# A graph layer with normalisation on one core: two of three row pairs turned by VectorE instead of every second one, block transfers issued from two queues, every sixth pair normalised by VectorE

## The chip, the core and the metric

The kernel runs on one core of one Trainium2 chip. The metric is the device time of one execution in microseconds, taken as the median of several runs. TensorE (PE in the profile), VectorE (DVE), ScalarE (ACT), GpSimd (POOL) and SyncE (SP) each follow an instruction queue of their own and meet only at semaphores. Data moves between HBM and the on-chip memory on 16 DMA engines.

## The reference, cut to what matters

There are 50,000 nodes with 512 float32 features. `src` and `dst` hold 62,500 edges sorted by `dst`: every node has a loop onto itself, and 12,500 edges join other nodes.

```
def _L0_gnn_ref(x, edge_index, W_l, W_r, b):
    src, dst = edge_index[0], edge_index[1]
    msg = x[src]
    agg = segment_sum(msg, dst, num_segments=n)
    deg = segment_sum(ones, dst, num_segments=n)
    mean = agg / maximum(deg, 1.0)[:, None]
    h = mean @ W_l + b + x @ W_r
    return h * sigmoid(h)
x = _layernorm(x + _L0_gnn_ref(x, (src, dst), W_l, W_r, b), axis=-1)   # eps 1e-5
```

A node whose only edge is its loop has mean = x, so that h = x @ (W_l + W_r) + b. For the others the kernel adds a correction row, computed from the differences x[src] - x[dst].

## The kernel before, in words

The rows are worked on in tiles of 128. The products are float32: the data and the weights are each split into a high and a low part of type float32r, and a tile of 128 rows takes 12 matmuls of 512 columns (four chunks of 128 features by three products, `three` at L529, issued at L535).

There are three stages. **Early** (to about 220 us): the products of the first 44 tiles (EARLY) are computed and kept in HBM, while VectorE sorts out which edges are not loops. **Edges** (to about 500 us): 98 tiles of correction rows (ET) are computed and written to HBM. **Node pairs** (from about 500 us): the other 347 tiles go by in 174 pairs (NP) of 256 rows, the last with 80 rows only. Between them the early tiles, called light, are finished, one for every four pairs.

All engines run a loop `node_pair(t)` (or `serve`, `move`) written out over t, with a fixed order of steps and with the steps of neighbouring pairs shifted against each other. For pair t:

- SP loads the rows into `X`, four buffers (`load_x`, L326), as soon as the residual of the pair four before has been added (`u_made`), and it stores the output (`store_out`, L344) when `normed` says so. `O` has two buffers, freed by `stored`.
- GpSimd gathers the correction rows of the pair into `cor`, four buffers (`gather_cor`, L468), over a bias that ScalarE has written there first (`reset_cor`, L747). Rows without a correction are skipped.
- The contracted feature must lie on the partitions, so x is turned. For even t TensorE does it: eight transposes of 128x128 into PSUM (`transpose_x`, L628, issued at L639), at the start of iteration t-1. For odd t VectorE does it in blocks of 32x32: SP loads the same rows a second time in another arrangement (`load_blocks`, L336: four DMAs, one for each 32 partitions, in runs of 128 elements, 512 bytes), into `x_raw`, and VectorE turns them into `x_blocks` with one instruction (`turn_blocks`, L1096). There is one buffer of each; both lie in `xs`, which the edge stage used for its gathers. The weights for these pairs have their rows in the matching order (`wb_hi`, `wb_lo`). `by_blocks` (L206) says which pair goes which way, and `turned_by_pe` (L209) counts the others.
- ScalarE rounds the turned rows to `x_hi` (`round_x`, L786: L792 from blocks, L796 from PSUM), and VectorE makes `x_lo` as the difference (`split_x`, L1083: L1088 and L1091).
- ScalarE copies the gathered corrections into PSUM (`seed`, L810), and TensorE accumulates 24 matmuls onto them.
- ScalarE applies SiLU from PSUM into `Z` (L833), VectorE adds X (`residual`, L1117) and takes mean and variance (`moments`, L1125 and L1128), GpSimd computes 1/sqrt(var + eps) (`make_rstd`, L502 and L505), VectorE makes -mean*rstd (`make_shift`, L1135), and ScalarE writes O = Z*rstd + shift in two instructions (`normalise`, L806).

The order in an iteration t on ScalarE is silu(t-1), round_x(t+1), seed(t+1), reset_cor(t+3), light steps, normalise(t-3); on VectorE moments(t-2), split_x(t+1), residual(t-1), make_shift(t-2), light steps, turn_blocks(t+2); on SP load_blocks(t+3), load_x(t+3), store_out(t-3), light transfers; on TensorE the transposes of t+1, then the 24 matmuls of t; on GpSimd a light rstd, make_rstd(t-2), gather_cor(t+3), a light gather.

## Time and profile before

| | |
|---|---|
| median of three runs | 1539.95 us (1539.58 to 1540.2) |
| the profiled execution, its own time | 1544.13 us |
| its span, first to last instruction | 1542.3 us |
| TensorE busy | 97% of the span |
| VectorE, ScalarE, GpSimd busy | 85%, 77%, 66% of the span |
| granted TensorE clock, mean | 0.993 |
| DMA | 397.68 MB, 258 GB/s over the span |

The profiled execution is one run of its own, 4.2 us longer than the median of the three others. Busy shares are means over three stages with different limits, so a change in the node stage is to be read from windows of that stage. TensorE's busy time counts matmuls from their start to a modelled end, and they overlap; the time from one to the next is shorter than the duration printed.

### The profile page before, as it was taken

How to read it: one execution, taken by the hardware profiler on the slowest of the kernel's cores; microseconds unless marked ns; L12 is line 12 of the kernel's file. 1: busy time of each engine (PE TensorE's matmuls, PEld its weight loads, DVE VectorE, ACT ScalarE, POOL GpSimd, SP SyncE). 2: the span in 40 equal slices, each digit the busy share in tenths (PEclk: the TensorE clock that was granted, in tenths of full speed). 3: DMA queues.
4: the chain of work that ended last, by engine and by line, in shares of the span. 5: the costliest groups of instructions: out<-in, count | busy, mean ns of one | idle time of the engine just before them, and what ended most of it. 6: DMA issues, size and time to landing. Idle time of an engine off the chain costs nothing.

```text
span 1542.3 us, 23969 instructions
## 1 busy us (share of the span) xinstructions
PE 1501.2 (97%) x7198; PEld 1241.7 (81%) x7198; DVE 1317.7 (85%) x2090; ACT 1180.2 (77%) x1603; POOL 1019.6 (66%) x1089
## 2 busy tenths in 40 slices
PE   7989999999999999999999999999999999999996
PEld 6868778887888778888888888888888888888885
DVE  7977999998998778888878888888888888888886
ACT  4444333433334689999999999999999999999997
POOL 6436556665662767777767767676777776777774
PEclk9999999999999999999999999999999999999998
DMA  5466588987898689999999999999999999999996
GB/s 192 149 209 196 173 248 256 272 257 241 266 266 250 182 254 292 275 285 282 272 266 275 287 289 270 282 287 273 285 276 279 276 277 282 286 268 284 279 279 199
DMA packets 299349, 397.68 MB, mean 258 GB/s; under 512 B 43036, under 2 KB 145206, under 8 KB 299221
## 3 DMA queue, kind: packets, MB, share of 16 engines
q1 hardware_dynamic: 251239, 321.43, 69.4%
q0 software_dynamic: 46944, 74.22, 17.8%
q8 instruction: 58, 0.95, 0.3%
q14 instruction: 70, 0.57, 0.1%
q10 hardware_dynamic: 1038, 0.50, 0.1%
HBM read 333.87 MB, written 139.67 MB: 307 GB/s over the span
## 4 chain that ended last, share of the span: by engine, by line
PE 68%; issue 9%; ACT 7%; DMA 6%; DVE 5%; POOL 3%; SPq 1%; POOLq 0%; ACTq 0%; DVEq 0%
PE pH L535 62%; DMA cor<-correction_rows,node_idx 3%; PE pT L639 3%; PE pT L608 2%; ACT cor L753 2%; ACT O L806 2%; POOL cor L441 1%; ACT pH L821 1%; ACT Z L833 1%; DMA xs<-in_x 1%; PE pT L546 1%; DVE stats L1125 1%; POOL var_eps L502 1%; SPq L310 1%; POOL rstd L505 1%
## 5 line engine op out<-in xcount | busy, mean ns | idle before, releaser
L441 POOL DMA_INDIRECT cor<-correction_rows,node_idx x347 | 397.5, 1146 | 242.9 <-ACT cor L753 144.3
L535 PE MATMUL pH<-ws_hi,x_hi 128*128 128x512 f32 x876 | 346.9, 396 | 5.8 <-ACT pH L821 2.0
L535 PE MATMUL pH<-ws_hi,x_lo 128*128 128x512 f32 x876 | 342.9, 391 | 0.0
L535 PE MATMUL pH<-ws_lo,x_hi 128*128 128x512 f32 x876 | 342.0, 390 | 0.0
L535 PE MATMUL pH<-wb_hi,x_hi 128*128 128x512 f32 x688 | 275.6, 401 | 1.4 <-DVE x_lo L1088 1.3
L535 PE MATMUL pH<-wb_hi,x_lo 128*128 128x512 f32 x688 | 268.2, 390 | 0.0
L535 PE MATMUL pH<-wb_lo,x_hi 128*128 128x512 f32 x688 | 267.8, 389 | 0.0
L806 ACT ACTIVATE O<-Z,shift,rstd 128x512 f32<-128x512 f32 x347 | 262.0, 804 | 2.0 <-DVE shift L1135 1.9
L1125 DVE BATCH_NORM_STATS2 stats<-Z 128x6 f32<-128x512 f32 x347 | 219.3, 673 | 0.0
L1117 DVE TENSOR_TENSOR Z<-Z,X 128x1024 f32<-128x1024 f32 x174 | 211.2, 1214 | 1.1 <-ACT Z L833 1.1
L727 ACT ACTIVATE s_hi<-sums 128x512 fp32r<-128x512 f32 x98 | 62.0, 633 | 189.9 <-issue 141.4
L535 PEld LDWEIGHTS pH<-ws_hi,x_hi 128*128 128x128 f32 x876 | 164.8, 188 | 43.0 <-issue 9.2
L535 PEld LDWEIGHTS pH<-ws_hi,x_lo 128*128 128x128 f32 x876 | 164.8, 188 | 35.2
L505 POOL TENSOR_TENSOR rstd<-var_eps,minus_half 128x2 f32<-128x2 f32 x174 | 183.3, 1054 | 14.5
L535 PEld LDWEIGHTS pH<-ws_lo,x_hi 128*128 128x128 f32 x876 | 165.1, 188 | 32.8
L833 ACT ACTIVATE Z<-pH 128x1024 f32<-128x1024 f32 x170 | 172.4, 1014 | 20.6 <-PE pH L535 18.6
L753 ACT ACTIVATE cor<-bias_rows 128x1024 f32<-128x1024 f32 x174 | 182.8, 1051 | 0.0
L821 ACT ACTIVATE pH<-cor 128x1024 f32<-128x1024 f32 x170 | 172.9, 1017 | 10.8 <-DMA cor<-correction_rows,node_idx 10.4
L1091 DVE TENSOR_TENSOR x_lo<-pT,x_hi 128x1024 fp32r<-128x1024 f32 x88 | 106.9, 1215 | 82.0 <-issue 56.7
L535 PE MATMUL pH<-wl_hi,s_hi 128*128 128x512 f32 x392 | 163.3, 417 | 2.7 <-DVE s_lo L1043 1.8
L441 POOL DMA_INDIRECT xd<-in_x,dst_idx x98 | 99.9, 1019 | 95.3 <-issue 69.6
L535 PE MATMUL pH<-wl_hi,s_lo 128*128 128x512 f32 x392 | 155.6, 397 | 0.0
(145 smaller groups left out, 2751.4 us busy)
## 6 DMA issues: line engine op xcount, KB each, us to landing
X<-in_x SPq DMA_DIRECT2D x173, 512.0 KB
out<-O SPq DMA_DIRECT2D x173, 512.0 KB
xs<-in_x SPq DMA_DIRECT2D x344, 128.0 KB
correction_rows<-c_out SPq DMA_DIRECT2D x98, 256.0 KB
light_x<-in_x SPq DMA_DIRECT2D x58, 256.0 KB, 2.8
light_h<-early_product SPq DMA_DIRECT2D x44, 256.0 KB
out<-light_o SPq DMA_DIRECT2D x44, 256.0 KB
join_row<-joined SPq DMA_DIRECT2D x98, 64.0 KB
```

The costliest lines, as they stand in the source:

```text
L441: g.indirect_dma_start(out=out_, out_offset=None, in_=table, in_offset=bass.IndirectOffsetOnAxis(ap=idx, axis=0), bounds_check=bound, oob_ ...
L505: g.tensor_tensor(rstd[0:rows, b, 0:nt], var_eps[0:rows, b, 0:nt], minus_half[0:rows, 0:nt], ALU.pow).then_inc(rstd_made, 1)
L535: last = mm(ps, a[:, k], w[:, k], start=(n == 0 and not onto), stop=(n == len(terms) - 1), skip_group_check=onto)
L639: last = nc.tensor.transpose(pT[u % 2][:, a, k * P:k * P + rows], X[0:rows, b, a, k * P:(k + 1) * P], eye[0:rows, 0:rows])
L727: a_(s_hi[b][:], sums[:, b, :, 2:], ACT.Copy).then_inc(s_hi_made, 1)
L753: a_(cor[u][:], bias_rows[:].rearrange("p (a n) -> p a n", a=1).to_broadcast([P, 2, D]), ACT.Copy).then_inc(cor_reset, 1)
L806: last = a_(O[0:rows, b, a], Z[0:rows, u % 4, a], ACT.Identity, scale=rstd[0:rows, b, a:a + 1], bias=shift[0:rows, b, a:a + 1])
L821: a_(pH[u % 2][0:rows, 0:nt], cor[b][0:rows, 0:nt], ACT.Copy).then_inc(seeded, 1)
L833: a_(Z[0:rows, b, 0:nt], h, ACT.Silu).then_inc(silu_made, 1)
L1091: v.tensor_tensor(x_lo[b][:, :, 0:nt, 0:rows].rearrange("p k a r -> p a k r"), pT[b][:, 0:nt].rearrange("p a (k r) -> p a k r", k=K)[:, :, ...
L1117: v.tensor_tensor(Z[0:rows, b, 0:nt], Z[0:rows, b, 0:nt], X[0:rows, b, 0:nt], ALU.add).then_inc(u_made, 1)
L1125: v.bn_stats(stats[0:rows, u % 2, a], Z[0:rows, u % 4, a]).then_inc(stats_made, 1)
```

## The change

1. Two of three pairs (t not a multiple of 3, and not the last) are turned by VectorE; the others and the last by TensorE.
2. `x_raw` and `x_blocks` have two buffers each, used in turn (`block_ring`); the second lies in `xd`, which becomes one tensor. `blocks_in` becomes two semaphores.
3. Of the four block DMAs of a pair, SP issues those of partitions 0 to 63, and ScalarE, between `seed` and `reset_cor`, those of partitions 64 to 127.
4. Pairs with t a multiple of 6 are normalised by VectorE, with (Z - mean) * rstd in two `tensor_scalar` instructions, ahead of `turn_blocks`; they need no shift. Some waits on `shift_made` and `rstd_made` become waits on `normed`.

```diff
@@ -91,8 +91,8 @@
         xs = sb("xs", [P, 4, D], f32)
-        x_raw, x_blocks = xs[:, 0:2], xs[:, 2:4]
-        xd = [sb(f"xd{b}", [P, D], f32) for b in range(4)]
+        xd = sb("xd", [P, 4, D], f32)
+        x_raw, x_blocks = (xs[:, 0:2], xd[:, 0:2]), (xs[:, 2:4], xd[:, 2:4])
         diff = [sb(f"diff{b}", [P, D], f32) for b in range(2)]
@@ -174,7 +174,7 @@
         cor_in = [sem(f"cor_in{b}") for b in range(4)]
-        blocks_in, blocks_turned = sem("blocks_in"), sem("blocks_turned")
+        blocks_in, blocks_turned = [sem(f"blocks_in{b}") for b in range(2)], sem("blocks_turned")
         transposed, hi_made, lo_made, product, z_made, silu_made = (sem("transposed"), sem("hi_made"), sem("lo_made"),
@@ -204,10 +204,28 @@
         def by_blocks(t):
-            return t % 2 == 1 and t < NP - 1
+            return t % 3 != 0 and t < NP - 1
         def turned_by_pe(t):
-            return t // 2 + 1 + t // (NP - 1)
+            return sum(not by_blocks(p) for p in range(t + 1))
+
+        def turned_by_dve(t):
+            return sum(by_blocks(p) for p in range(t + 1))
+
+        def block_ring(t):
+            n = turned_by_dve(t) - 1
+            return n % 2, n // 2
+
+        def normed_by_dve(t):
+            return t % 6 == 0
+
+        def shifts(t):
+            return sum(not normed_by_dve(p) for p in range(t + 1))
+
+        def block_part(t, j):
+            first = BASE + 2 * t * P
+            return (x_raw[block_ring(t)[0]][32 * j:32 * j + 32].rearrange("r a (i c) -> r (a i) c", i=4),
+                    x[first:first + 2 * P, j * P:(j + 1) * P].rearrange("(i r) c -> r i c", r=32))
@@ -334,12 +352,9 @@
             def load_blocks(t):
-                wait(sp, blocks_turned, (t + 1) // 2 - 1)
-                first = BASE + 2 * t * P
-                for j in range(4):
-                    sp.dma_start(x_raw[32 * j:32 * j + 32].rearrange("r a (i c) -> r (a i) c", i=4),
-                                 x[first:first + 2 * P, j * P:(j + 1) * P].rearrange("(i r) c -> r i c", r=32)
-                                 ).then_inc(blocks_in, 16)
+                wait(sp, blocks_turned, turned_by_dve(t) - 2)
+                for j in range(2):
+                    sp.dma_start(*block_part(t, j)).then_inc(blocks_in[block_ring(t)[0]], 16)
@@ -379,6 +394,7 @@
                     load_blocks(1)
+                    load_blocks(2)
             peeled(0, ET, edge_tile)
@@ -497,7 +513,6 @@
                 wait(pool, mv_made, 2 * t + 2)
-                wait(pool, shift_made, t - 1)
                 wait(pool, normed, t - 1)
@@ -631,8 +646,8 @@
                 pe.wait_ge(x_in[b], 16 * (used + 1))
-                if fixed(t) and t < 2:
-                    pe.wait_ge(sums_made, ET - 1 + t)
+                if fixed(t) and t < 4:
+                    pe.wait_ge(sums_made, min(ET - 1 + t, ET))
                 wait(pe, lo_made, t - 1)
@@ -788,8 +803,8 @@
                 if by_blocks(t):
-                    act.wait_ge(blocks_turned, (t + 1) // 2)
-                    a_(in_blocks(x_hi[b]), x_blocks.rearrange("p a (i k r) -> p (a i) k r", k=K, r=32), ACT.Copy
+                    act.wait_ge(blocks_turned, turned_by_dve(t))
+                    a_(in_blocks(x_hi[b]), x_blocks[block_ring(t)[0]].rearrange("p a (i k r) -> p (a i) k r", k=K, r=32), ACT.Copy
                        ).then_inc(hi_made, 1)
@@ -797,11 +812,19 @@
+            def load_blocks(t):
+                wait(act, blocks_turned, turned_by_dve(t) - 2)
+                for j in range(2, 4):
+                    act.dma_start(*block_part(t, j)).then_inc(blocks_in[block_ring(t)[0]], 16)
+
             def normalise(t, q, u):
+                if normed_by_dve(t):
+                    return
                 nt, rows = pair_shape(t)
                 b, used = ring(q, u, 2)
-                wait(act, shift_made, t + 1)
+                wait(act, shift_made, shifts(t))
                 wait(act, stored[b], 16 * used)
+                wait(act, normed, t)
                 for a in range(nt):
@@ -849,6 +872,9 @@
             single(0, round_x)
+            act.wait_ge(diff_made, ET)
+            load_blocks(1)
+            load_blocks(2)
@@ -859,6 +885,8 @@
                     shifted(t, q, u, 1, NP, seed)
+                if by_blocks(t + 3):
+                    load_blocks(t + 3)
                 shifted(t, q, u, 3, NP, reset_cor)
@@ -1085,7 +1113,7 @@
                 if by_blocks(t):
-                    v.tensor_tensor(in_blocks(x_lo[b]), x_blocks.rearrange("p a (i k r) -> p (a i) k r", k=K, r=32),
+                    v.tensor_tensor(in_blocks(x_lo[b]), x_blocks[block_ring(t)[0]].rearrange("p a (i k r) -> p (a i) k r", k=K, r=32),
                                     in_blocks(x_hi[b]).bitcast(f32), ALU.subtract).then_inc(lo_made, 1)
@@ -1094,10 +1122,10 @@
             def turn_blocks(t, q, u):
-                dve.wait_ge(blocks_in, 64 * ((t + 1) // 2))
-                if t > 1:
-                    dve.wait_ge(lo_made, t - 1)
-                v.transpose(x_blocks, x_raw).then_inc(blocks_turned, 1)
+                b, used = block_ring(t)
+                dve.wait_ge(blocks_in[b], 64 * (used + 1))
+                wait(dve, lo_made, t - 2)
+                v.transpose(x_blocks[b], x_raw[b]).then_inc(blocks_turned, 1)
@@ -1120,7 +1148,10 @@
                 wait(dve, u_made, t + 1)
-                wait(dve, rstd_made, t - 1)
+                if t > 1 and normed_by_dve(t - 2):
+                    dve.wait_ge(normed, t - 1)
+                else:
+                    wait(dve, rstd_made, t - 1)
                 for a in range(nt):
@@ -1128,12 +1159,27 @@
             def make_shift(t, q, u):
+                if normed_by_dve(t):
+                    return
                 nt, rows = pair_shape(t)
...
                                        ALU.mult, ALU.mult).then_inc(shift_made, 1)
+
+            def normalise(t, q, u):
+                if not normed_by_dve(t):
+                    return
+                nt, rows = pair_shape(t)
+                b, used = ring(q, u, 2)
+                wait(dve, stored[b], 16 * used)
+                wait(dve, rstd_made, t + 1)
+                wait(dve, normed, t)
+                for a in range(nt):
+                    last = v.tensor_scalar(O[0:rows, b, a], Z[0:rows, u % 4, a], mv[0:rows, b, a, 0:1],
+                                           rstd[0:rows, b, a:a + 1], ALU.subtract, ALU.mult)
+                last.then_inc(normed, 1)
@@ -1180,6 +1226,7 @@
                 lights(light, t)
+                shifted(t, q, u, -3, NP, normalise)
                 if by_blocks(t + 2):
...
             peeled(0, NP, node_pair)
```

## Rows read from the trace of the kernel before

**Rows 1.** By stretch: busy us of PE, PEld, DVE, ACT, POOL; granted clock; DMA share; GB/s.

```profile
560.00:580.00 20.00, 17.93 (x82) 14.35 (x81) 15.20 (x27) 16.37 (x21) 12.11 (x15) 1.00 0.82 235
...
1000.00:1023.56 23.56, 23.56 (x114) 19.68 (x113) 19.89 (x36) 22.68 (x28) 16.33 (x20) 1.00 0.95 278
...
1500.00:1520.00 20.00, 20.00 (x98) 16.72 (x97) 16.67 (x30) 19.70 (x24) 14.67 (x15) 1.00 0.87 256
```

**Rows 2.** Chain of waits around the start of the full stretch: start, us, what.

```profile
555.49 8.12 DMA cor<-correction_rows,node_idx
...
577.19 5.71 PE pH L535 x24
582.90 0.87 PE pT L639 x8
583.77 10.90 PE pH L535 x48
```

**Rows 3.** TensorE transposes of the whole run, by line.

```profile
L639 PE MATMUL pT<-eye,X x700: 231/272/275, 496.5 to 1520.9; 128*128 128x128 f32 x174, 80*128 80x80 f32 x1
```

**Rows 4.** VectorE groups, 1000 to 1094.24 us (sixteen pairs): busy us, mean ns, idle before.

```profile
L1125 DVE BATCH_NORM_STATS2 stats<-Z 128x6 f32<-128x512 f32 x32 | 20.2, 672 | 0.0
L1117 DVE TENSOR_TENSOR Z<-Z,X 128x1024 f32<-128x1024 f32 x16 | 19.5, 1217 | 0.0
L1091 DVE TENSOR_TENSOR x_lo<-pT,x_hi 128x1024 fp32r<-128x1024 f32 x9 | 11.0, 1225 | 10.0 <-ACT x_hi L796 6.9 <-issue 3.1
L1100 DVE STREAM_TRANSPOSE xs<-xs 128x1024 f32<-128x1024 f32 x8 | 9.8, 1231 | 0.0
L1088 DVE TENSOR_TENSOR x_lo<-xs,x_hi 128x1024 fp32r<-128x1024 f32 x8 | 9.7, 1209 | 2.4 <-ACT x_hi L792 2.4
...
L1135 DVE SCALAR_TENSOR_TENSOR shift<-mv,rstd 128x2 f32<-128x2 f32 x16 | 2.5, 155 | 3.3 <-POOL rstd L505 3.3
```

**Rows 5.** Tensor-scalar instructions of VectorE in the whole run, by shape.

```profile
L903 DVE TENSOR_SCALAR cor<-cor 128x512 int32<-128x512 int32 x9 | 6.7, 745 | 0.3
...
L903 DVE TENSOR_SCALAR row_mask<-X 128x512 int32<-128x512 int32 x1 | 0.4, 429 | 0.0
```

**Rows 6.** ScalarE groups, 1000 to 1094.24 us: busy us, mean ns, idle before.

```profile
L806 ACT ACTIVATE O<-Z,shift,rstd 128x512 f32<-128x512 f32 x32 | 24.2, 805 | 0.0
...
L821 ACT ACTIVATE pH<-cor 128x1024 f32<-128x1024 f32 x16 | 16.3, 1022 | 0.0
```

**Rows 7.** Timeline of the ACT queue at the start: start, us, what.

```profile
1.10 0.46 ACTq L685 DMA_DIRECT2D cor<-in_dst  x1
1.59 0.70 ACTq L688 DMA_DIRECT2D cor<-in_dst  x1
```

**Rows 8.** Block transfers issued by the SP queue, timeline: start, us, what.

```profile
1004.51 2.13 SPq L340 DMA_DIRECT2D xs<-in_x  x4
...
1014.44 3.17 SPq L340 DMA_DIRECT2D xs<-in_x  x4
```

**Rows 9.** Waits of the SP queue, 577 to 1518 us: total, times, longest.

```profile
SPq L331 <- DVE Z L1117: 350.6, 146, 4.6
```

**Rows 10.** DMA by queue, 1018 to 1019 us: packets, MB, share of 16 engines.

```profile
q1 hardware_dynamic: 440, 0.22, 99.7%
```

**Rows 11.** The same, 1019 to 1020 us.

```profile
q1 hardware_dynamic: 349, 0.18, 104.2%
```

**Rows 12.** The same, 1002 to 1003 us.

```profile
q1 hardware_dynamic: 30, 0.06, 37.1%
```

**Rows 13.** The same, 1016 to 1017 us.

```profile
q1 hardware_dynamic: 186, 0.37, 98.9%
```

**Rows 14.** The same, 1000 to 1023.56 us (four pairs).

```profile
q1 hardware_dynamic: 4780, 6.02, 86.8%
q0 software_dynamic: 714, 0.49, 7.7%
```

**Rows 15.** ScalarE waiting for gathers, 700 to 1500 us: total, times, longest.

```profile
ACT pH L821 <- DMA cor<-correction_rows,node_idx: 6.2, 6, 2.8
```

More of the change, by code:

```diff
@@ L34, in gnn_layer @@
     assert (NTILES - EARLY) % 2 == 1 and ET % 2 == 0 and NP % 2 == 0 and COLS <= 512
-    assert 4 * EARLY == NP + 2
+    assert 4 * EARLY == NP + 2 and all((NP - n) % 6 for n in (1, 2, 3))
     LATE = 28
@@ L447, in gather_xd @@
                 wait(pool, diff_made, t - 3)
-                gather(xd[u][:], x, dst_idx[:, t:t + 1], P, N - 1, xd_in[u])
+                gather(xd[:, u], x, dst_idx[:, t:t + 1], P, N - 1, xd_in[u])
             def gather_xs(t, q, u):
@@ L1025, in subtract @@
                 wait(dve, turned, t - 1)
-                v.tensor_tensor(diff[b][:], xs[:, r], xd[r][:], ALU.subtract).then_inc(diff_made, 1)
+                v.tensor_tensor(diff[b][:], xs[:, r], xd[:, r], ALU.subtract).then_inc(diff_made, 1)
             def scan(t, q, u):
```

## The prediction

> **What bounds the kernel now.** The stretches of the profile come first [rows 1]. From about 580 us to about 1518 us TensorE is busy for the whole of every window at a granted clock of 1.00, and ScalarE for 22.68 of 23.56 us, VectorE for 19.89; the DMA share is 0.95. Several things look full, so the chain of waits decides: from 577.19 us it holds nothing but matmuls and TensorE's transposes [rows 2]. 48 matmuls take 10.90 us, so a pair's 24 take 5.45; eight transposes take 0.87. The pattern of two pairs is 10.90 + 0.87 = 11.78 us, four pairs last 23.56, one 5.89, and about (1518 - 577) / 5.89 = 160 pairs go by like that. The first 14 (500 to 577 us) and the drain at the end do not: there the chain has gathers and ScalarE, as in the 8.12 us gather [rows 2], and TensorE has gaps (17.93 busy of 20 us [rows 1]).
>
> So in the full stretch only TensorE's own work counts, as long as the others keep below it. The others' limits are close, and the question is who passes it.
>
> **TensorE.** The 700 transposes [rows 3] are 87 pairs of eight and four for the last. Afterwards 58 full pairs and the last are turned there: 29 pairs fewer, 29 x 0.87 = 25.2 us. Of these 160 / 6 = 26.7 pairs, 23.2 us, lie in the full stretch; the other 2.0 us lie in the start, where something else ends last, and I count 1 of them, giving 24. Three pairs now take 3 x 5.45 + 0.87 = 17.2 us, so four take 22.96. That is the limit which the rest must keep to. No matmul is added: the pairs that change sides use the other set of weights, in the same number.
>
> **VectorE, for four pairs.** It turns 2.67 pairs instead of 2: 0.67 x 1.23 = 0.8 us [rows 4]. The x_lo of a pair costs 1.21 us from blocks and 1.23 from PSUM [rows 4]: nothing. Normalising 0.67 pairs takes two instructions each of a form that the trace lacks. Its nearest rows are one-source instructions on 128x512 four-byte values, 429 ns and 745 ns [rows 5], so a pair costs 0.86 to 1.49 us. I take 0.9, since the row of 429 also goes from SBUF to SBUF and its two constants stand for the two scalars here; together 0.6, at most 1.0. The shifts save 0.1. Sum: 19.9 + 0.8 + 0.6 - 0.1 = 21.2 us, at most 21.6, of 22.96: hidden. Its iteration with t = 3 mod 6 holds turning and normalising together: moments 1.7, x_lo 1.2, residual 1.2, transpose 1.2 [rows 4], normalise 0.9 to 1.5, and in some iterations a light step of 0.7 (as one 512-column instruction of L1125) make 6.9 to 7.5 us against 5.45. The next iteration has no turning and gives it back; the idle time ahead of x_lo (10.0 us over nine, 1.1 each [rows 4]) is the cover. The worst case lacks 7.5 - 5.45 - 1.1 = 0.9 us once in six pairs, 27 x 0.9 = 24 us if nothing cushions it; but TensorE wants x_lo(t+1) only when it is through with pair t, so I count nothing. If that cover is gone, TensorE waits for x_lo.
>
> **ScalarE, for four pairs.** It loses 0.67 normalisations of 24.2 / 16 = 1.51 us [rows 6]: 22.68 - 1.0 = 21.7 of 22.96. It gains 2.67 x 2 = 5.3 DMA issues. The trace has no such issue in the stage; at the start one takes 0.46 us in ScalarE's queue, another 0.70 [rows 7], and a group of four on SP takes 2.13 to 3.17 us, 0.53 to 0.79 each [rows 8]. Below: nothing, if the queue issues them while the engine works through the seed ahead (1.02 us [rows 6]), which is dispatched first. Above: all of it, 5.3 x 0.5 = 2.7 us, and 24.3 us for four pairs. I take nothing, since the queue's records and the engine's are separate and two issues of 0.46 to 0.5 us fit under one seed. A wait stands before the issues, on VectorE's turning of the pair three before; that lies two iterations back, so it is met. What is queued behind it are the reset of `cor` and the normalisation. SP is relieved of the same 5.3 issues and gets 1.3 new; it idles 350.6 us in waits for the residual alone [rows 9].
>
> **DMA, for four pairs.** 0.67 more block loads, each 1024 packets of 512 bytes. Such packets take 16 x 0.997 / 440 = 36 ns in one window [rows 10] and 16 x 1.042 / 349 = 48 ns in the next [rows 11]; a load is 2.3 to 3.1 us of all 16 engines, and the addition 1.5 to 2.0. Now 0.95 x 23.56 = 22.4 us are taken. The sum, 23.9 to 24.4, is above 22.96. But the share counts packets as busy while they wait: after the queue has run empty they take 16 x 0.371 / 30 = 198 ns [rows 12], in full flow 16 x 0.989 / 186 = 85 ns [rows 13]. Built from flowing packets, four pairs are 2432 of 2 KB (four X, four out, three light) x 85 / 16 = 12.9 us, 2731 of 512 bytes at 36 to 48, 6.1 to 8.2, and gathers 0.077 x 23.56 = 1.8 [rows 14]: 20.8 to 22.9. The two bounds lie on either side of the limit. I take the lower, because SP's loads now wait for buffers and not for engines [rows 9], and because the window of the empty queue shows room. It is the weakest step, and I give 2 us over the stage for transfers that come late: gathers already make ScalarE wait 6.2 us, six times, up to 2.8 [rows 15].
>
> The row that speaks for a short packet is [rows 10], and the order of the transfers may help: partitions 0 to 63 come from one queue and 64 to 127 from another. By that, the trace agrees: 349 and 440 packets of 512 bytes in 1 us [rows 10, 11] are 179 to 225 GB/s, where 2 KB packets reach 370 [rows 13]. No row here shows two halves at once.
>
> **Sum.** 24 - 2 = 22 us off. The profiled execution took 1544.1, so it would take 1522; the median of the runs shown is 4.2 lower, so I forecast 1518. Its own range is 1513 (all 25.2, and 2 from the start) to 1528.
>
> **Rivals.**
>
> *DMA becomes the bound (slower).* Place: the 16 engines in the full stretch. Decided where the packets of four pairs need more than 22.96 us; slower where they need more than 23.56. With 23.9 to 24.4 us it is (0.34 to 0.84) x 40 = 14 to 34 us more: 1554 to 1574. For it: queue shares of 1.00 and more in the windows with blocks [rows 10, 11]. Against it: the 198 ns packets, and the waits of the SP queue [rows 9, 12]. Chance 0.14. The Trainium skill, DMA: Bandwidth & Descriptors, "Issuing engines are not separate DMA queues", says that issuing from more engines saves only the issue time; by that the second queue leaves the packets at the 48 ns of [rows 11], the upper end of both sums.
>
> *ScalarE pays for its issues (slower).* Decided from (22.96 - 21.7) / 5.3 = 0.24 us exposed for each issue. Fully exposed, 24.3 us, x 40: 30 us more, 1570. [...] Against it: the cover of the seed. Chance 0.09.
>
> *Half is eaten.* VectorE's heavy iteration, late gathers or part of either rival cost 10 to 20 us: 1528 to 1537. Chance 0.13.
>
> *No difference:* the new limit lands at the old one; it needs a coincidence. Chance 0.04. *The transposes do not leave:* excluded by the count, since `by_blocks` governs both TensorE's steps and the weights.
>
> **Numbers.** Forecast 0.60, half eaten 0.13, none 0.04, DMA 0.14, ScalarE 0.09. A measurement of this kernel tells about 0.2%, 3.1 us, from no change. Faster 0.73, same 0.04, slower 0.23. The range is 1512 to 1556: it takes in the forecast, the half and the start of the DMA case, and leaves out most of the slower ones.
>
> **What would show it.** Right: TensorE at 20.00 of 20 us in the stretch, 17.2 us for three pairs in its chain, 468 transposes, x_raw loads in the ACT queue under the seed's time, and a smaller mean time for 512-byte packets. Wrong: gaps on TensorE ahead of matmuls that wait for x_lo or a seed; SP waiting on `stored` or TensorE on X (DMA); idle ScalarE after the issues (the second rival); POOL slower, its 1/sqrt held up by VectorE's new instructions and the shift late. A span under 1510 would mean that the start gained as well.

## The result, and the profile after

The changed kernel takes 1578.4 us, the median of four runs (1576.23 to 1581.37); the kernel before took 1539.96 beside it. The ratio is 1.0254 [1.0234, 1.0273], with the 95% interval in brackets as everywhere below: 2.5% slower, where 1.4% faster was forecast. The profiled execution took 1579.75 us, its span is 1578.0, at a mean granted clock of 0.993, the same as before.

The windows of the kernel after, with the columns of [rows 1]: first the stretch of 23.56 us of [rows 1], then the 800 us on which all readings below rest.

```profile
1000.00:1023.56 23.56, 22.15 (x100) 17.63 (x99) 19.88 (x36) 19.95 (x24) 19.18 (x19) 1.00 1.01 292
...
700.00:1500.00 800.00, 763.97 (x3468) 618.24 (x3467) 692.26 (x1183) 702.87 (x834) 622.99 (x618) 1.00 0.97 282
```

The same 800 us of the kernel before:

```profile
700.00:1500.00 800.00, 799.53 (x3801) 667.34 (x3800) 674.94 (x1187) 767.77 (x917) 576.11 (x645) 1.00 0.96 279
```

TensorE was busy for all of it and now has 36 us of gaps, at an unchanged granted clock of 1.00. ScalarE lost work, as it should. GpSimd, to which the change gives no instruction, rose from 576 to 623 us, and it did so for fewer pairs. The pairs in a window can be counted by the residual's instruction: 136 before, 131 after, so that a pair takes 5.88 and 6.11 us. 0.23 us over 160 pairs are 37 us, nearly all of the 38 us lost.

GpSimd's groups in the 800 us, busy us, mean ns and idle before them, of the kernel before:

```profile
L505 POOL TENSOR_TENSOR rstd<-var_eps,minus_half 128x2 f32<-128x2 f32 x136 | 141.2, 1038 | 11.3
L502 POOL TENSOR_SCALAR var_eps<-mv 128x2 f32<-128x2 f32 x135 | 64.6, 478 | 19.3 <-DVE mv L1128 16.0 <-issue 0.4
```

and of the kernel after:

```profile
L520 POOL TENSOR_TENSOR rstd<-var_eps,minus_half 128x2 f32<-128x2 f32 x131 | 166.7, 1273 | 10.9
L517 POOL TENSOR_SCALAR var_eps<-mv 128x2 f32<-128x2 f32 x131 | 96.6, 738 | 25.1 <-DVE mv L1159 21.5
```

These instructions work on 128x2 values and were not edited. Together they went from 1.52 to 2.01 us a pair. A timeline of the kernel *before* shows what makes them long or short; start, duration, what. Here VectorE works on a pair that was turned in blocks:

```profile
1004.71 1.19 DVE L1088 TENSOR_TENSOR x_lo<-xs,x_hi 128x1024 fp32r<-128x1024 f32 x1
...
1004.97 1.02 POOL L502 TENSOR_SCALAR var_eps<-mv 128x2 f32<-128x2 f32 x1
...
1005.82 1.22 DVE L1117 TENSOR_TENSOR Z<-Z,X 128x1024 f32<-128x1024 f32 x1
...
1006.07 1.54 POOL L505 TENSOR_TENSOR rstd<-var_eps,minus_half 128x2 f32<-128x2 f32 x1
```

and here, one pair later, the other way was taken, through PSUM:

```profile
1010.01 1.23 DVE L1091 TENSOR_TENSOR x_lo<-pT,x_hi 128x1024 fp32r<-128x1024 f32 x1 [0.62 <-issue]
...
1010.26 0.23 POOL L502 TENSOR_SCALAR var_eps<-mv 128x2 f32<-128x2 f32 x1
...
1010.57 0.72 POOL L505 TENSOR_TENSOR rstd<-var_eps,minus_half 128x2 f32<-128x2 f32 x1
```

VectorE's two forms of `x_lo` last about equally long (1.19 and 1.23 us), but the one from blocks has both its inputs in SBUF and the other has one in PSUM. Beside the first, GpSimd's `var_eps` ends only when VectorE's instruction does (1005.99, 1005.90); beside the second it takes 0.23 us. GpSimd's 1/sqrt is then pushed beside the residual, again an instruction with two SBUF inputs, and lasts 1.54 us instead of 0.72. The Trainium skill, SBUF — State Buffer, "Who interferes with whom", says just that: a VectorE instruction with two SBUF inputs contends with a GpSimd instruction that reads SBUF, and one with at most one SBUF input doesn't, outside the modes in which VectorE uses both of its port pairs for one input. The trace agrees: 1.02 against 0.23 us.

All pairs of the 800 us say the same, sorted by what VectorE was running when GpSimd's instruction began (times, mean us):

| | `var_eps`, before | `var_eps`, after | 1/sqrt, before | 1/sqrt, after |
|---|---|---|---|---|
| `x_lo` from blocks | 38, 1.05 | 74, 0.88 | 9, 1.67 | 11, 1.64 |
| the residual | 3, 0.97 | 21, 1.10 | 42, 1.55 | 75, 1.55 |
| `x_lo` from PSUM | 65, 0.23 | 24, 0.23 | 62, 0.72 | 23, 0.72 |
| transposes, or nothing | 29, 0.22 | 12, 0.22 | 23, 0.72 | 22, 0.72 |

So `var_eps` began beside an instruction with two SBUF inputs in 41 of 135 cases before and in 95 of 131 after, 1/sqrt in 51 of 136 and in 86 of 131. That is more than the blocks alone bring: 21 `var_eps` now begin so late that they meet the residual.

The change makes the first form the rule, in two of three pairs. The waits of the kernel after in the 800 us; total, times, longest:

```profile
POOL cor L457 <- ACT cor L768: 66.2, 44, 4.2
DVE shift L1168 <- POOL rstd L520: 57.0, 86, 1.8
...
ACT x_hi L807 <- DVE xd L1128: 49.4, 31, 3.7
ACT pH L844 <- DMA cor<-correction_rows,node_idx: 33.6, 22, 4.3
...
PE pH L550 <- DVE x_lo L1116: 16.9, 23, 1.0
PE pH L550 <- ACT pH L844: 16.7, 21, 3.2
```

The last two are 33.6 of TensorE's 36 us of gaps. Before, the seed waited 6.2 us for gathers [rows 15], and the other two waits were:

```profile
DVE shift L1135 <- POOL rstd L505: 30.0, 46, 1.8
...
ACT x_hi L792 <- DVE xs L1100: 6.8, 14, 0.9
```

How one leads to the other is to be seen in the chain of waits of the kernel after, from 1018.51 us (start, us, what):

```profile
1018.51 1.26 DVE stats L1156 x2
...
1020.13 1.12 POOL var_eps L517
1021.25 0.07 issue
1021.32 1.54 POOL rstd L520
...
1022.89 0.04 DVE shift L1168
...
1023.07 1.26 DVE xd L1128
...
1024.41 0.04 ACT x_hi L807
```

Statistics, held `var_eps`, held 1/sqrt, shift, turning, rounding. The shift stands ahead of turning in VectorE's queue, so VectorE idles (0.60 us here) with the blocks already there, and ScalarE waits for the turned rows. A second path leaves from the same place: GpSimd's gathers stand behind the held instructions, come late, and hold the seed. In the chain of waits over the 800 us, GpSimd's own instructions are 30% of the kernel after, and the landing of its gathers 12%; before, they were 2% and 5%.

### The profile page after: what moved, and what is told of

Read it like the earlier page. It is cut to its first block, busy times and chain, and to the rows that moved or that the text cites. A ratio compares the mean times of both kernels' runs of the same rounds, so it can differ in the third digit from the quotient of the medians.

```text
span 1578.0 us, 23593 instructions
## 1 busy us (share of the span) xinstructions
PE 1494.5 (95%) x6966; PEld 1214.0 (77%) x6966; DVE 1375.4 (87%) x2148; ACT 1137.2 (72%) x1545; POOL 1103.5 (70%) x1089
## 4 chain that ended last, share of the span: by engine, by line
PE 25%; POOL 20%; issue 17%; ACT 14%; DVE 11%; DMA 10%; ACTq 2%; SPq 1%; POOLq 0%; DVEq 0%
PE pH L550 21%; DMA cor<-correction_rows,node_idx 9%; POOL cor L457 6%; POOL rstd L520 6%; POOL var_eps L517 5%; ACT O L829 4%; ACT cor L768 3%; POOL light_cor L457 3%; PE pT L623 2%; DVE stats L1156 2%; ACTq L818 2%; DVE xd L1128 2%; ACT light_z L860 1%; ACT light_cor L773 1%; DVE l_stats L1197 1%
## 5 line engine op out<-in xcount | busy, mean ns | idle before, releaser
L550 PE MATMUL pH<-wb_hi,x_hi 128*128 128x512 f32 x920 | 368.1, 400 | 46.0 <-ACT pH L844 22.2
L550 PE MATMUL pH<-wb_hi,x_lo 128*128 128x512 f32 x920 | 360.1, 391 | 0.0
L550 PE MATMUL pH<-wb_lo,x_hi 128*128 128x512 f32 x920 | 359.2, 390 | 0.0
L550 PE MATMUL pH<-ws_hi,x_hi 128*128 128x512 f32 x644 | 257.1, 399 | 3.3 <-DVE ws_lo L921 2.6
L550 PEld LDWEIGHTS pH<-wb_hi,x_hi 128*128 128x128 f32 x920 | 173.0, 188 | 103.9 <-issue 69.8
L550 PE MATMUL pH<-ws_hi,x_lo 128*128 128x512 f32 x644 | 252.5, 392 | 0.0
L550 PE MATMUL pH<-ws_lo,x_hi 128*128 128x512 f32 x644 | 252.0, 391 | 0.0
L550 PEld LDWEIGHTS pH<-wb_hi,x_lo 128*128 128x128 f32 x920 | 173.0, 188 | 37.2
L550 PEld LDWEIGHTS pH<-wb_lo,x_hi 128*128 128x128 f32 x920 | 173.3, 188 | 33.1
L457 POOL DMA_INDIRECT xd<-in_x,dst_idx x98 | 99.7, 1018 | 88.3 <-DVE diff L1054 85.2
L517 POOL TENSOR_SCALAR var_eps<-mv 128x2 f32<-128x2 f32 x174 | 124.8, 717 | 41.5 <-DVE mv L1159 36.7
```

The source lines that it names most:

```text
L457: g.indirect_dma_start(out=out_, out_offset=None, in_=table, in_offset=bass.IndirectOffsetOnAxis(ap=idx, axis=0), bounds_check=bound, oob_ ...
L517: g.tensor_scalar(var_eps[0:rows, b, 0:nt], mv[0:rows, b, 0:nt, 1], EPS, None, ALU.add).then_inc(eps_added, 1)
L550: last = mm(ps, a[:, k], w[:, k], start=(n == 0 and not onto), stop=(n == len(terms) - 1), skip_group_check=onto)
```

## The experiments

Kernels of one group ran on one chip beside the kernel before; its median was 1543.75, 1537.7, 1538.78, 1539.69 and 1543.51 us in the five groups, so ratios are compared and not times. The kernel after was not run again beside them: its 1.0254 comes from its own group, and differences of 0.2% or less between groups are not told apart.

### Group 1: each part of the change, and the eps

**The issues.** All four block transfers of a pair by SP again.

```diff
-                for j in range(2):
+                for j in range(4):
...
-                if by_blocks(t + 3):
-                    load_blocks(t + 3)
                 shifted(t, q, u, 3, NP, reset_cor)
```

> The changed kernel with all four block DMAs of a pair issued by SP again, none by ScalarE. Theory P (GpSimd and VectorE hold each other up: slow 1/sqrt, late shift, late turning): no change within 5 us of 1578, since neither engine does less. Theory D (the DMA engines are full): the same or up to 15 us slower, since the 512-byte packets of one half after the other take longer. Theory S (ScalarE pays for its issues, 230 of them): 1578 - 230 x 0.1 to 0.4 = 1486 to 1555, bounded below by TensorE's 1515.

Measured 1584.3 us, 1.0259 [1.0238, 1.028]: no difference. The run takes away ScalarE's issues and the second queue at once, so it shows only that the two together change nothing here. That the issues cost little is to be seen in one stretch of ScalarE's timeline of the kernel after:

```profile
1024.41 1.06 ACT L807 ACTIVATE x_hi<-xd 128x1024 fp32r<-128x1024 f32 x1 [0.46 <-DVE xd L1128]
1024.53 1.32 ACTq L818 DMA_DIRECT2D xs<-in_x  x2
1025.38 1.01 ACT L844 ACTIVATE pH<-cor 128x1024 f32<-128x1024 f32 x1
1026.33 1.05 ACT L768 ACTIVATE cor<-bias_rows 128x1024 f32<-128x1024 f32 x1
```

The queue issues while the engine works on the instructions in front; even two issues that take 1.32 us together leave no gap ahead of the reset of `cor`.

**Normalisation.** ScalarE normalises every pair (`normed_by_dve` returns False).

> The changed kernel with every pair normalised by ScalarE. VectorE does 29 x 1.0 us less, ScalarE 29 x 1.5 more. Theory P: VectorE's heavy iteration is lighter, 5 to 25 us faster. Theory D: no change within 5 us. Theory S: ScalarE is the fuller engine, so slower by 20 us or more.

1569.19 us, 1.0163 [1.0141, 1.0185]. VectorE's normalisation was a loss of 0.9%. Its waits go with that: the rounding for turned rows falls from 49.4 + 12.7 us to 17.0 + 14.3, while the shift's wait stays (61.8). GpSimd's two instructions stay held (762 and 1238 ns), so VectorE's normalisation is not what holds them. 14 of the 38 us came with this part, and the rest did not.

**Block loads.** They are made for the first pairs only, and later turns use what lies in the buffers (in both `load_blocks`, SP's and ScalarE's).

```diff
+                if t > 2:
+                    return
...
-                dve.wait_ge(blocks_in[b], 64 * (used + 1))
+                dve.wait_ge(blocks_in[b], 64)
```

> The changed kernel with the block transfers made only for the first use of each of the two buffers; the later pairs of these buffers turn old data (this leaves out 113 block loads of 512 KB, and the output is not that of the reference). Theory D: the stage falls back to TensorE's limit, 1510 to 1525. Theory P: at most 15 us faster, 1563 to 1578, since only the gathers land sooner. Theory S: as D, since ScalarE's issues go too; e1 tells D and S apart.

1568.2 us, 1.0153 [1.0131, 1.0174]. The DMA share fell to 0.70, and 15 us came off; 1.5% of loss stayed with the DMA engines a third idle. They are not the bound here.

**The eps.** GpSimd takes the power of the bare variance: one instruction, one semaphore and one chance of being held less for each pair.

```diff
-                g.tensor_scalar(var_eps[0:rows, b, 0:nt], mv[0:rows, b, 0:nt, 1], EPS, None, ALU.add
-                                ).then_inc(eps_added, 1)
-                pool.wait_ge(eps_added, t + 1)
-                g.tensor_tensor(rstd[0:rows, b, 0:nt], var_eps[0:rows, b, 0:nt], minus_half[0:rows, 0:nt], ALU.pow
+                g.tensor_tensor(rstd[0:rows, b, 0:nt], mv[0:rows, b, 0:nt, 1], minus_half[0:rows, 0:nt], ALU.pow
```

> The changed kernel without the addition of eps ahead of the 1/sqrt of the pairs (leaves out eps = 1e-5 there). GpSimd does one instruction of 0.72 us less for each pair. Theory P: the loop over GpSimd and VectorE shortens by up to 0.8 us a pair of 5.9 to 6.1, down to 1520 to 1550. Theory D and S: no change within 5 us.

1549.84 us, 1.0042 [1.0026, 1.0057]: 33 us off by taking away an instruction that works on two values a row. It is the largest gain of any single edit to the kernel after, level with the return to every second pair below. Every other engine's instructions are the same.

### Group 2: is it the eps alone, and the shift's place

**The shift last.** VectorE's order becomes residual, turning, light step, normalisation, shift, so turning no longer stands behind the wait for 1/sqrt.

```diff
                 shifted(t, q, u, -1, NP, residual)
-                shifted(t, q, u, -2, NP, make_shift)
-                lights(light, t)
-                shifted(t, q, u, -3, NP, normalise)
                 if by_blocks(t + 2):
                     single(t + 2, turn_blocks)
+                lights(light, t)
+                shifted(t, q, u, -3, NP, normalise)
+                shifted(t, q, u, -2, NP, make_shift)
```

> The changed kernel with VectorE's order altered: in an iteration the turning comes right behind the residual, and the shift, which waits for GpSimd's 1/sqrt, last. No instruction more or less. Theory P1 (the loss lies in VectorE standing still for the shift, with the turning queued behind it: 57.0 us of waits in 800, 70 in the stage of 950): 20 to 40 us faster, 1540 to 1558. Theory P2 (the loss lies in GpSimd's own load, 4.8 us of instructions and 1 us of gaps for a pair of 6.1): less than 10 us faster, 1568 to 1578. Theory D (DMA): no change.

1572.64 us, 1.0235 [1.0215, 1.0255]: no difference clear of noise, where the expectation's first theory wanted 20 to 40 us. Yet the edit did what it should. Of its waits:

```profile
ACT pH L844 <- DMA cor<-correction_rows,node_idx: 71.5, 45, 3.6
...
DVE shift L1168 <- POOL rstd L520: 13.4, 27, 0.8
```

The shift's wait fell from 57.0 to 13.4 us, and the seed's wait for gathers rose from 33.6 to 71.5. One cover had been taken off another. The theory that the shift's place was the cause fell with this run, in the form that it was the only one.

**The kernel before without the eps.**

> The kernel before without the addition of eps on GpSimd in the pairs (leaves out eps = 1e-5 there). Theory P: before, TensorE bounds the stage and GpSimd has room, so no change: within 3 us of the kernel before. If it is faster by over 5 us, GpSimd was a bound already and the run without eps of the changed kernel proves less.

1535.21 us, 0.9979 [0.9969, 0.9989]. The same edit that gives 2.1% after gives 0.2% before, where TensorE stays busy for 799.39 of 800 us: GpSimd's time was nearly free there and isn't any more.

**No eps, and blocks loaded once.**

> The changed kernel with both reliefs: no addition of eps on GpSimd, and blocks loaded only for the first use of each buffer (leaves out eps and 113 block loads). With the blocks alone left out it took 1568, without eps alone 1550 with a DMA share of 1.00. Theory P then D (two limits one behind the other): both together reach TensorE's limit, 1512 to 1525. If GpSimd alone matters: 1545 to 1550 as without eps.

1522.33 us, 0.9901 [0.9885, 0.9918], TensorE busy for 796.10 of 800 us. With GpSimd lighter the loads are worth 1.4% (1.0042 to 0.9901, two chips), with its full work 1.0%: more of their cost shows once the other wait is gone.

**Two of three pairs and two buffers alone**, with SP's issues and ScalarE's normalisation.

> The changed kernel with two of three pairs turned by VectorE and the two buffers, but all block DMAs issued by SP and every pair normalised by ScalarE. Theory P: VectorE and GpSimd are as in the run with ScalarE's normalisation (1569), the DMA issues add the 6 us they did in the run with SP alone: 1570 to 1580. Theory S (ScalarE's issues cost): faster than 1565.

1568.47 us, 1.0202 [1.0185, 1.0219]. The core of the change loses 2.0% by itself. Against 1.0163 of the kernel that also issues from ScalarE (another chip), the second queue with ScalarE's issues is worth 0.4% here, with intervals that touch at 1.0185, though the same step was worth nothing beside VectorE's normalisation.

### Group 3: keeping the held instructions clear of VectorE

**Moments behind the residual.** VectorE's order becomes x_lo, residual, moments, turning, light step, normalisation, shift: now turning, with one source, stands beside `var_eps` and 1/sqrt.

```diff
-                shifted(t, q, u, -2, NP, moments)
                 shifted(t, q, u, 1, NP, split_x)
                 shifted(t, q, u, -1, NP, residual)
-                shifted(t, q, u, -2, NP, make_shift)
-                lights(light, t)
-                shifted(t, q, u, -3, NP, normalise)
+                shifted(t, q, u, -2, NP, moments)
                 if by_blocks(t + 2):
                     single(t + 2, turn_blocks)
+                lights(light, t)
+                shifted(t, q, u, -3, NP, normalise)
+                shifted(t, q, u, -2, NP, make_shift)
```

> The changed kernel with VectorE's order altered and nothing else: x_lo, residual, moments, turning, light, normalise, shift. GpSimd's two 1/sqrt instructions then run beside the transposes (one input from SBUF) and not beside x_lo and the residual (two inputs each). If GpSimd's instructions are held up by VectorE's two-input ones: var_eps falls from 738 ns to about 240, the 1/sqrt from 1273 to about 750, 1 us a pair; the time falls to 1540 to 1555, where the DMA share is full, as without eps (1550). If they are slow for another reason: both durations stay, and so does the time, as with the shift last (1573).

1643.92 us, 1.0671 [1.0642, 1.0701]: much slower, where 1540 to 1555 us was expected, and the most telling miss. GpSimd's groups:

```profile
L520 POOL TENSOR_TENSOR rstd<-var_eps,minus_half 128x2 f32<-128x2 f32 x123 | 88.2, 717 | 10.2
L517 POOL TENSOR_SCALAR var_eps<-mv 128x2 f32<-128x2 f32 x123 | 34.0, 276 | 186.6 <-DVE mv L1159 186.5
```

and its waits:

```profile
POOL var_eps L517 <- DVE mv L1159: 186.5, 111, 4.7
...
ACT pH L844 <- DMA cor<-correction_rows,node_idx: 78.7, 37, 4.3
...
PE pH L550 <- ACT pH L844: 57.3, 22, 3.3
```

The collision is gone: 276 and 717 ns instead of 738 and 1273, which also prices it, at 1.02 us a pair in the kernel after and 0.52 in the kernel before. But GpSimd now waits 186.5 us for the mean and variance, and its gathers stand behind that wait: the seed comes late and TensorE waits for it. GpSimd's queue being late is what counts, whether it is held or kept waiting. The granted clock of the 800 us is 0.97 here and not 1.00, so part of the loss, by estimate up to 3% of TensorE's time, is the clock's.

**The same with ScalarE normalising every pair.**

> The order of the run before this one, with every pair normalised by ScalarE. If DMA is the limit that comes next: the same within 5 us, as neither engine is full. If VectorE's load counts still: 5 to 15 us faster. If ScalarE is full: slower.

1655.76 us, 1.075 [1.0725, 1.0775]; `var_eps` waits 200.4 us. VectorE's relief does not help: the kernel is 0.8% slower still, at a granted clock of 0.98 in the 800 us.

**The same with three of five pairs turned by VectorE.**

> Three of five pairs turned by VectorE, VectorE's order of the first run of this group, all pairs normalised by ScalarE, transfers issued by both queues. TensorE's limit is 5.45 + 0.87 x 2/5 = 5.80 us a pair, 15 us below the kernel before; block loads are 0.6 a pair instead of 0.5 or 0.67. If the DMA limit grows with the block loads, this lies between: 1525 to 1540, and may beat both kernels.

1641.69 us, 1.0666 [1.0629, 1.0703]. Turning fewer pairs gives 0.8% of it back, far from the 1525 to 1540 us expected; the waits are the same (199.8 us for `mv`).

**Every second pair, as before, with the rest of the change.**

> The changed kernel with every second pair turned by VectorE, as before; two buffers, transfers issued by both queues and VectorE's normalisation of every sixth pair stay. Theory P: the share of turned pairs is what loads GpSimd and the DMA, so this falls back to the kernel before: 1535 to 1550. If the other parts of the change cost something by themselves: over 1550.

1548.37 us, 1.0051 [1.0036, 1.0065]. So of the 2.5%, the 29 more pairs bring 2.0, and buffers, issues and normalisation 0.5 by themselves. TensorE is busy for 797.27 of 800 us here.

### Group 4: gathers one pair further ahead

**Gathers ahead.** Reset and gather are made for pair t+4 instead of t+3; the four buffers of `cor` allow it.

```diff
-                shifted(t, q, u, 3, NP, gather_cor)
+                if t <= ADDED:
+                    shifted(t, q, u, 3, NP, gather_cor)
+                if t >= ADDED:
+                    shifted(t, q, u, 4, NP, gather_cor)
```

(and the same for `reset_cor`).

> The changed kernel with the correction rows reset and gathered one pair earlier (for pair t+4 in iteration t, from t = 4 on; the buffer is free by then). No instruction more or less. Theory G (the latency of reset, gather, landing and seed loses the time): 20 to 50 us faster, 1525 to 1558. Theory T (GpSimd's throughput, 5.4 us with its gaps for a pair of 6.1): within 8 us of 1578. Theory D (DMA full): within 8 us.

1567.61 us, 1.0177 [1.016, 1.0194]. Of its waits:

```profile
ACT x_hi L810 <- DVE xd L1134: 65.9, 32, 3.4
DVE shift L1174 <- POOL rstd L520: 54.0, 83, 0.9
```

The seed's wait for gathers has gone from the list, and the rounding waits longer for turned rows (49.4 before the edit). It is the mirror of the shift's run: each edit alone takes one wait away and meets the other.

**Gathers ahead, blocks loaded once.**

> As the run before this one, with the blocks loaded only for the first use of each buffer (leaves out 113 block loads). Theory G with D as the next limit: 1515 to 1530, TensorE's limit. Theory G with another limit (VectorE waits for the shift): little below the run before, 1535 or more.

1562.99 us, 1.0157 [1.014, 1.0174]. The loads are worth 0.2% now, within the intervals, and against 1.0153 without the edit, gathers ahead bring nothing: in all three runs the seed's wait for gathers is gone from the list. Leaving the loads out and gathering earlier cure the same thing, gathers that come late.

**Gathers ahead, moments late, ScalarE normalising.**

> The gathers one pair earlier, VectorE's order of e12 (moments behind the residual, shift last) and all pairs normalised by ScalarE. e13 was this without the earlier gathers: 1656. Theory G: about 100 us faster than e13, 1535 to 1560. If x_lo or the turning is what is late there: over 1600.

1554.26 us, 1.0103 [1.0086, 1.012], from 1.075 without gathers ahead: 6.5% came from gathers queued behind the wait, with what the granted clock lost by TensorE's gaps (0.98 there, 1.00 here). GpSimd waits 145.3 us for `mv` still, and TensorE is busy for 783.59 of 800 us all the same.

**The kernel before with gathers ahead.**

> The kernel before with the gathers one pair earlier. TensorE bounds its stage, so within 4 us of the kernel before; at best the start of the stage, where an 8 us gather stands in the chain, gains a few.

1537.41 us, 0.9986 [0.9976, 0.9995]. 2 us came back. What this run tells of the trace before is said under "Why the prediction was wrong".

### Group 5: both waits taken away

**Gathers ahead and the shift last**: the two edits shown above, on the kernel after.

> The changed kernel with the gathers one pair earlier and VectorE's shift last, behind the turning; no work left out or added. Alone, the first gave 10 us and the second 3 to 5, as each uncovered the other's wait. If the two waits cover each other: 1545 to 1556, with a DMA share of about 1.00 and TensorE waiting for X, as without eps. If GpSimd's throughput is the limit: over 1562.

1526.32 us against 1543.51, 0.9905 [0.9876, 0.9933]. This is the whole change with nothing left out, 1% faster than the kernel before, 3.4% faster than the kernel after and faster than the 1545 to 1556 us expected. Its window and its waits:

```profile
700.00:1500.00 800.00, 793.63 (x3674) 657.14 (x3673) 730.14 (x1254) 747.83 (x884) 655.99 (x651) 1.00 1.00 298
```

```profile
DVE xd L1134 <- DMA xd<-in_x: 20.6, 20, 1.9
DVE shift L1174 <- POOL rstd L520: 20.3, 35, 0.6
PEld pT L657 <- DMA X<-in_x: 12.2, 16, 1.8
...
ACT x_hi L810 <- DVE xd L1134: 5.3, 9, 1.1
```

The edits bring 0.8% and 0.2% (the second not clear of noise) of the kernel before's time alone and 3.5% together. 138 pairs go by in 800 us, 5.80 us each. GpSimd is still held (its two instructions take 1.89 us a pair); what changed is who stands behind them. What remains are waits for block and row loads, and in the chain 7.0% for stores of the output, at a DMA share of 1.00.

**The same with three of five pairs.**

> The same with three of five pairs turned by VectorE instead of two of three. Block loads are 0.6 a pair instead of 0.67 (0.07 x 2.3 to 3.1 us = 0.15 to 0.2 us of the engines less), TensorE's limit is 5.80 us instead of 5.74. If DMA is the remaining limit: 20 to 30 us faster than the run before this one, 1522 to 1535, and so faster than the kernel before. If VectorE or GpSimd is: within 10 us of the run before this one.

1526.77 us, 0.9896 [0.9878, 0.9914]: the same time, where 20 to 30 us less was expected if transfers were what remained. It is reached otherwise. TensorE is busy for 798.37 of 800 us, and its matmuls and transposes are 82.4% of the chain in these 800 us; in the run before this one the matmuls are 8.2% of it and transfers in and out 20%. With three fifths of the pairs turned TensorE is mostly the bound; with two thirds, waits for transfers take as much as was saved.

## Why the prediction was wrong

**What held.** TensorE's part did: 468 transposes instead of 700 [rows 3], as counted, and the limit of 5.74 us a pair was neared, at 5.80, once only transfers were late. VectorE's own work for four pairs is 692.26 / 131 x 4 = 21.1 us, forecast 21.2; the normalising instruction took 549 ns, 1.1 us a pair, within the 0.86 to 1.49 given and above the 0.9 taken. ScalarE's issues cost nothing that shows, as taken, and its rival falls with the first run: 30 us would have come back. The DMA rival came nearest in time, 1554 to 1574, for the wrong reason: with the loads left out the kernel is still 1.5% slower than before, and with all of them 1.0% faster. The step that took the lower of two bounds, 20.8 to 22.9 us, was right that a share near 1 is no limit by itself, but its size was too small: a mean packet of 2 KB took 99 ns in the 800 us before, not 85, and four pairs keep the engines busy for 1.00 x 5.80 x 4 = 23.2 us in the kernel with gathers ahead and the shift last. The argument for the second queue by ports compared packets of 512 bytes with those of 2 KB, so it could not show the ports; packets became 12% shorter and the kernel no faster (last section). And SP is relieved of 4 issues in four pairs, not 5.3, which no sum used.

**The step that failed** is the one for VectorE and what it left out: "The x_lo of a pair costs 1.21 us from blocks and 1.23 from PSUM: nothing." The durations were right (about 1210 and 1217 ns in the groups after), and "nothing" was wrong, because the instruction was priced by its own time and not by what it does to the engine beside it. It exchanges one SBUF input for two, and GpSimd's two small instructions grow from 1.52 to 2.01 us a pair. With that goes what the prediction left out altogether: it had no term for GpSimd. That engine was read as busy for two thirds of the time and so as free, while its queue feeds two consumers with little slack, the shift and the gathers. The trace of before had it: the shift's wait of 3.3 us in sixteen pairs stands in [rows 4], and the collision was there in 41 of 135 `var_eps` and 51 of 136 1/sqrt. The text named it as a sign that would show the forecast wrong ("its 1/sqrt held up by VectorE's new instructions and the shift late"), and gave it neither a price nor a chance. As a rival it would have had its place, and a price from rows: in one more pair of six (1.02 - 0.23) + (1.54 - 0.72) = 1.6 us, 0.27 us a pair. Measured were 0.5, since GpSimd's instructions also began later and met the residual more often.

**The reading of the chain behind it** failed too: "from 577.19 us it holds nothing but matmuls and TensorE's transposes". [rows 2] show it for the start of the stretch only. In the same trace the chain leaves TensorE at 730.60 us for 83 us, and from 1344 us it does not touch TensorE up to 1500:

```profile
725.13 5.47 PE pH L535 x24
...
733.44 1.05 ACT cor L753
...
742.88 1.01 POOL cor L441
...
744.83 1.00 POOL var_eps L502
...
749.06 7.70 DMA cor<-correction_rows,node_idx
```

Reset, gather, held `var_eps`, landing and seed took as long there as TensorE took for its pairs. TensorE hardly waited for them (0.5 us in the 800), yet in these 240 of 800 us they had next to nothing to spare, so that less work for TensorE alone would have gained little there. With gathers ahead the kernel before has a chain that is TensorE's alone in the 800 us, at 0.9986 of the time: the second loop had been as long as the first and had cost next to nothing.

**"So I count nothing"** for VectorE's heavy iteration failed as well. The cover was the idle time ahead of `x_lo`. It was 66.7 + 17.1 us in 800 us before and is 17.6 + 13.4 after, since the work added and the longer waits for the shift have eaten it. Turning stands behind the shift in consecutive iterations now, where before a turn was always followed by an iteration without one. The worst case was put at 0.9 us once in six pairs, 24 us; the run without VectorE's normalisation gives 14.

**Where the expected gain went**: TensorE's 24 us did leave; but a pair takes 6.11 us against its limit of 5.74, and 0.37 x 160 = 59 us of waits took their place. By the runs, they stand behind GpSimd, on two paths that cover each other, so that no split into shares adds up: 3 and 12 us alone, 54 together. That GpSimd came later because it was held is argued from the durations; VectorE's heavier iterations, which the 14 us show, are mixed with it. Why the second queue is worth 0.4% in one setting and nothing in another is open, as is how much of the 0.5% of the kernel with every second pair belongs to which part. A kernel in which GpSimd's instructions stand clear of VectorE's and `mv` is early as well was not found, so what the collision alone costs was not measured apart from lateness; taking one of the two held instructions away gives 33 us.

## What to carry to other kernels

Price an instruction that changes where its inputs lie also by what runs beside it on GpSimd, and look up the duration of GpSimd's smallest instructions for both forms. An engine at 66% is free only if nothing queued behind its held or waiting instructions is due soon: list for each engine what its queue feeds, with the slack of each. Follow the chain of waits through the whole stretch and not its first windows: where it leaves the engine that looks full, a second loop is as long. When one edit moves a wait and gains nothing, look which wait has grown instead, and take both away before dropping either.

## What the runs showed of the hardware

GpSimd's 128x2 instructions last 0.23 and 0.72 us beside a VectorE instruction with one SBUF input and 1.02 and 1.54 us beside one with two; beside VectorE's transposes and statistics they last 0.22 and 0.72 us (with moments behind the residual). VectorE's own instruction is not lengthened: `x_lo` from blocks takes 1208 ns on the mean before, the one from PSUM 1224.

The two queues with block transfers overlap at the DMA engines. One window of the kernel after, from 1009 to 1010 us, by queue (packets, MB, share of 16 engines):

```profile
q10 hardware_dynamic: 302, 0.15, 52.9%
q1 hardware_dynamic: 205, 0.10, 33.5%
q0 software_dynamic: 39, 0.03, 12.8%
```

That is 16 x 0.529 / 302 = 28 ns and 16 x 0.335 / 205 = 26 ns a packet, at 282 GB/s, against 36 and 48 ns from one queue [rows 10, 11]. Single windows differ; over the 800 us the mean packet of 512 bytes took 41.8 ns before, 40.2 with all block transfers issued by SP, and 35.2 in the kernel after. The Trainium skill, DMA: Bandwidth & Descriptors, "Issuing engines are not separate DMA queues", says that only issue time is saved; the rows show shorter packets as well, and the measured time shows no gain from them in this kernel (1.0254 against 1.0259), and 0.4% without VectorE's normalisation.

A DMA share of 0.96 was no limit: 279 GB/s went with it before, and 298 GB/s at 1.00 in the kernel with gathers ahead and the shift last.
